# Two message-passing layers on one core: a new opening, wider one-hots, longer rings and VectorE operands in PSUM

## The chip, the cores and the metric

The kernel runs on one core of one Trainium2 chip. The metric is the device time of one execution in microseconds (us), from the start of the program to its end. Of the kernel before, three timed runs and one profiled execution are at hand.

## The reference, cut to what matters

The graph has 12500 nodes of 128 features and 412500 edges, sorted by target. Two layers run one after the other:

```python
deg = maximum(segment_sum(ones, dst), 1.0); d = deg ** -0.5
h = maximum(layernorm(x), 0.0)
msg = where(edge_type == 0, h[src] @ W_data.T + b_data, h[src] @ W_control.T + b_control)
x = x + relu(segment_sum(msg, dst) + h @ W_self.T + b_self)
h = maximum(layernorm(x), 0.0)
g = tanh((h @ gate_w[:D])[dst] + (h @ gate_w[D:])[src] + gate_b)
yn = tanh(edge_weight * yes_weight + (1 - edge_weight) * no_weight)
x = x + segment_sum(h[src] * ((g + yn) * 0.5 * d[dst] * d[src])[:, None], dst)
```

## The kernel before, in words

**Opening.** The nodes are 98 blocks of 128, in 14 chunks of 7 blocks (`CB`). SyncE (SP) loads the chunks of x, and between them the targets (after chunk 2) and the sources (after chunk 3) of the edges, and later their types. For each chunk VectorE takes mean and variance (`stats`), turns them into a scale and a shift (`scales`, L1195, whose L1199 reads two small SBUF tensors), ScalarE applies them (`normal`), TensorE transposes the chunk (`turn`), ScalarE takes the positive part into `HTB`, TensorE multiplies by the self weights (`strip(2)`, L878) and by the two message weights (`strip(4, 256)`, L883), ScalarE puts the self term into the accumulator `ACC` (L664), and VectorE adds the biases into the message rows `YB` (`rows`, L1187, behind `stats` by four chunks). SP stores a chunk of rows to the table `t0` in HBM, and behind each the self terms to `ini`. `YB` has two buffers, so the rows of chunk c wait until those of chunk c - 2 have landed. GpSimd meanwhile computes the indices of the edges (L534 to L562), then waits for the last rows of `t0` and begins to gather.

**Gathers.** An edge tile is 128 edges. Of the 3224 tiles the last 2112 or so are gathered one by one: one indirect DMA issued by GpSimd (L570) brings 128 rows of the table to a ring `G` of 5 slots of 8 tiles. Each layer has 251 items of 8 tiles in a main loop (2008 gathers) and 13 more items (`sections`, 104 gathers) behind it. Before item s GpSimd waits until TensorE has used item s - 5.

**Cells.** The other 1112 tiles are served in another way, in 18 groups of 98 cells (`NG`, `NB`). A cell is a block of 128 source nodes against a window of 256 targets. SP loads the table's rows two cells at a time into a ring (`TC`, `TC1`, 4 places, `RT`) and a row of codes (`RB0`, `RB1`). VectorE compares the codes with the partition number (`pair_hots`, L1290, two operations of 256 columns for two cells; `pair_hots1`, L1747, one of them) and TensorE gathers with that one-hot (`gather`, `gather1`). ScalarE brings the result to SBUF. VectorE makes the one-hot of the targets (`cell_hots`, L1300; `target_hots1`, L1768, two cells in one operation), and TensorE adds the cell into a group's sum (`apply`, `apply1`; in layer 2 in two banks of PSUM in turn), which VectorE adds to `ACC` (L1283, L1787). In layer 2 VectorE also picks for each cell the target's score (`target_score`, L1760: the targets' one-hot times a piece of `ACC`, with an accumulated sum). The constant 0 to 255 that these compare with is `IO16`, int16 in SBUF.

**Items.** For each gathered item VectorE makes a one-hot of 8 x 32 columns (`item_hot`, L1251; `hot1`, L1688, two buffers). In layer 1 it adds the four tiles of a quad for the counts in two steps (L1258, L1260); the `sections` do this by one reduction (L1550). In layer 2 it multiplies the one-hot by scores (L1699), reduces (L1706), adds the source's score (L1715, which waits for the gather), and after ScalarE's tanh weights the one-hot (L1725, L1729). TensorE multiplies, and VectorE adds 32 columns at a time to `ACC` (L1274, L1741).

The order of an engine's work is written out by hand: for each item s, a loop over i mixes the cells `CELL[s]` to `CELL[s+1]` (7 an item) with the item's own steps. Between the layers and at the end the sums are transposed and stored.

Of the kernel before, what the change touches and what calls it, by code (L numbers as in the profile page):

```python
# [5 lines left out]
N = 12500  # L6
D = 128
# [17 lines left out]
NC = NB // CB  # L25

# [26 lines left out]
RT = 4  # L53
# [4 lines left out]
KD1, KX1, KW1 = 6, 6, 8  # L58
# [38 lines left out]
def gnn_program(nc, x, src, dst, d0, g0, typ, ew, w2, ws, bb, bs, gwr, gs, gb, yw, nw, out):  # L97
# [17 lines left out]
    with ctx:  # L115
# [27 lines left out]
        OHT = sb("OHT", [128, TG // QT, 2, W], bf16)  # L143
# [36 lines left out]
        EE = sb("EE", [128, 2, TG])  # L180
        PS = ctx.enter_context(nc.psum_tensor("PS", [128, 8, 512], fp32))
# [4 lines left out]
        def strip(bank, w=128):  # L186
# [24 lines left out]
        HTE += 64 * HB * RT  # L211
        MVF = MV[:, :, :].rearrange("p b a -> p (b a)")
# [8 lines left out]
        OT0 = [a.bitcast(bf16).rearrange("p (a w) -> p a w", a=2)  # L221
               for a in (W2[:, :], OHF[:, 1792:2048], YN[:, HTE:HTE + 256])]
        CD0 = CDST[:, 0:KD * DW // 2].bitcast(bf16).rearrange("p (a w) -> p a w", a=KD)
        OHU = [a[:, 0:2 * NB].bitcast(bf16) for a in (BB, MVF)]
        HTE += 256
# [8 lines left out]
              for a in (HTB[:, :, :, :].rearrange("p a c d -> p (a c d)"), OWF) for n in range(2)]  # L234
# [43 lines left out]
        c_t, c_o = sems("c_t", "c_o")  # L278
# [37 lines left out]

        def passes0(eng):
# [19 lines left out]
        def units(slot, ring=RT):  # L337

            return -(-(NH - slot) // ring)

        def parts_in(c):

            return 16 * units(c % RT) + 32 * (c // RT + 1)

        def pairs_in(c):

            return 16 * units(c % RT) + 32 * (-(-(NG * NH - c % RT) // RT) + c // RT + 1)
# [20 lines left out]
        def _(eng):  # L368
# [3 lines left out]
            for c in range(NC):  # L372
# [6 lines left out]
                if c == 2:  # L379
                    load(STI, dst, s_dst)  # L380
                if c == 3:
                    load(IDX[:, :], src, s_src)
            for c in range(NC):
                if c == 4:
# [3 lines left out]
                eng.wait_ge(a_ye, c + 1)  # L388
# [1494 lines left out]
```

## Time and profile before

| what | value |
|---|---|
| median of 3 runs | 5841.05 us (5840.38 to 5857.13) |
| the profiled execution | 5829.9 us, its span 5828.1 us |
| opening, to the first gather | 0 to 124.4 us |
| layer 1, main loop of gathers | 124.4 to about 2701 us |
| its sections | to about 2853 us |
| between the layers | to about 2963 us |
| layer 2, main loop of gathers | 2963 to about 5628 us |
| its sections, and the end | to 5828 us |
| busy in layer 1 (2576.6 us) | PE 2055.5, DVE 1984.9, ACT 1570.2, POOL 1964.9 us |
| busy in layer 2 (2665.1 us) | PE 1929.8, DVE 2089.7, ACT 1312.9, POOL 2052.2 us |

Busy time of POOL is the time of its instructions; the time between two DMA issues of POOL is written "issue". A stretch's busy time says how full an engine is, not whether the end waits for it. That is read from the waits and from the chain of work that ended last.

### The profile page before, as it was taken

Reading aid. Unit: us, or ns where it says so; the run is one execution under the profiler, and the core shown is the slowest. Engines: PE = TensorE matmul, PEld = TensorE weight load, DVE = VectorE, ACT = ScalarE, POOL = GpSimd, SP = SyncE. Lnnn points to the kernel's source line nnn. Section 1 sums busy time; section 2 is a strip of 40 time slices with the busy share of each in tenths; the row PEclk is TensorE's granted clock in tenths of the full one; section 3 lists DMA queues with packets and bytes.
Section 4 is the critical chain, followed back from the end, with each engine's and each line's share of the span. In section 5 each row is a group of like instructions: output and inputs, shape, how many; then the busy total and the mean of one; then the engine's idle time right before and its main releaser. Section 6 shows DMA issues by size and latency. Waiting matters only on the chain.

```text
span 5828.1 us, 119944 instructions
## 1 busy us (share of the span) xinstructions
PE 4286.3 (74%) x29542; PEld 3197.4 (55%) x29542; DVE 4365.5 (75%) x16525; ACT 3038.4 (52%) x10494; POOL 4307.3 (74%) x4285
## 2 busy tenths in 40 slices
PE   6588888888888888875577777777777777777754
PEld 5355666655565555553455555555555555555543
DVE  7887777878787777755467777777777777777863
ACT  5666666666666666643254544544445444444530
POOL 5777777777777777777457777777777777777774
PEclk8599999999999999987688888888888888888875
DMA  7777777777777777776355455555555455455544
GB/s 239 245 217 223 222 224 223 225 221 223 225 225 224 223 223 222 220 224 203 102 134 121 118 118 119 121 119 120 119 119 121 119 119 119 118 120 118 120 97 116
DMA packets 764988, 979.91 MB, mean 168 GB/s; under 512 B 135667, under 2 KB 567063, under 8 KB 763799
## 3 DMA queue, kind: packets, MB, share of 16 engines
q1 hardware_dynamic: 620131, 687.26, 40.0%
q0 software_dynamic: 135168, 281.42, 19.7%
q8 instruction: 259, 4.24, 0.3%
q10 hardware_dynamic: 9012, 3.56, 0.2%
q14 instruction: 418, 3.42, 0.2%
HBM read 911.05 MB, written 60.67 MB: 167 GB/s over the span
## 4 chain that ended last, share of the span: by engine, by line
POOL 72%; issue 23%; PE 2%; DVE 2%; DMA 1%; SPq 1%; ACTq 0%; DVEq 0%; POOLq 0%; ACT 0%
POOL G L570 72%; SPq L311 1%; PE PS L883 0%; DMA OWF<-in_x 0%; DMA out<-OWF 0%; DVE ST L1172 0%; DVE OHF L1183 0%; DVE G L1639 0%; PE PS L891 0%; DMA G<-t,IDXB 0%; PE PS L1054 0%; PE PS L1057 0%; DVE OWF L1191 0%; DVE OWF L1832 0%; PE PS L1081 0%
## 5 line engine op out<-in xcount | busy, mean ns | idle before, releaser
L570 POOL DMA_INDIRECT G<-t,IDX x4016 | 4019.1, 1001 | 1274.3 <-issue 1223.0
L1081 PE MATMUL PS<-CDST,HTB 128*128 128x256 f32 x2352 | 868.3, 455 | 447.7 <-DVE CDST L1768 419.9
L705 ACT ACTIVATE OHF<-PS 128x384 bf16<-128x384 f32 x1764 | 864.6, 490 | 515.7 <-PE PS L927 488.0
L939 PE MATMUL PS<-CDST,OHF 128*128 128x256 bf16 x5292 | 901.0, 281 | 35.0 <-DVE ACC L1283 35.0
L797 ACT ACTIVATE ST<-PS,MV 128x1 f32<-128x1 f32 x1764 | 457.5, 259 | 720.2 <-issue 327.6
L1072 PE MATMUL PS<-HTB,OWF 128*128 128x129 f32 x3528 | 815.1, 317 | 9.7 <-DVE OWF L1747 9.7
L1072 PEld LDWEIGHTS PS<-HTB,OWF 128*128 128x128 f32 x3528 | 720.5, 218 | 166.8 <-issue 75.9
L1081 PEld LDWEIGHTS PS<-CDST,HTB 128*128 128x128 f32 x2352 | 408.0, 217 | 556.0 <-ACT HTB L816 510.4
L939 PEld LDWEIGHTS PS<-CDST,OHF 128*128 128x128 bf16 x5292 | 532.6, 101 | 315.8 <-issue 68.7
L1081 PE MATMUL PS<-OHF,OWF 128*128 128x256 f32 x1176 | 438.6, 459 | 246.5 <-DVE OHF L1768 230.2
L1300 DVE TENSOR_SCALAR CDST<-IO,BASE 128x256 bf16<-128x256 int16 x1764 | 510.8, 305 | 5.0 <-PE PS L939 4.1
L808 ACT ACTIVATE ST<-ST,BASE 128x1 f32<-128x1 f32 x1764 | 501.1, 284 | 3.0
L958 PE MATMUL PS<-PAY,OWF 128*128 128x196 f32 x1484 | 408.8, 362 | 55.3 <-DVE OWF L1352 47.5
L1760 DVE SCALAR_TENSOR_TENSOR W<-IO,BASE,ACC 128x256 f32<-128x256 int16 x882 | 423.4, 480 | 9.8 <-ACT ST L797 2.9
L816 ACT ACTIVATE HTB<-PS,ST 128x128 f32<-128x128 f32 x1176 | 419.2, 356 | 0.1
L1760 DVE SCALAR_TENSOR_TENSOR BB<-IO,BASE,ACC 128x256 f32<-128x256 int16 x882 | 417.8, 474 | 0.6
L1715 DVE TENSOR_TENSOR SS<-DD,G 128x8 f32<-128x8 f32 x251 | 43.7, 174 | 483.1 <-issue 475.7
L1768 DVE TENSOR_TENSOR CDST<-IO,BASE 128x512 f32<-128x512 int16 x588 | 403.3, 686 | 0.0
L900 PE MATMUL PS<-G,OHF 128*32 128x128 f32 x4016 | 183.5, 305 | 283.0 <-DMA G<-t,IDX 262.8
L1747 DVE TENSOR_SCALAR OWF<-OHF,PCODE 128x256 f32<-128x256 int16 x882 | 347.1, 394 | 36.6 <-DMA HTB<-t 28.8
L1081 PEld LDWEIGHTS PS<-OHF,OWF 128*128 128x128 f32 x1176 | 207.1, 220 | 299.5 <-ACT OWF L816 275.5
L712 ACT ACTIVATE YN<-PS 128x128 f32<-128x128 f32 x251 | 69.7, 278 | 457.8 <-PE PS L906 390.3
(240 smaller groups left out, 8316.9 us busy)
## 6 DMA issues: line engine op xcount, KB each, us to landing
HTB<-t0s SPq DMA_DIRECT2D x442, 384.0 KB
OWF<-t0s SPq DMA_DIRECT2D x440, 384.0 KB
HTB<-t SPq DMA_DIRECT2D x882, 132.0 KB
G<-t,IDX POOLq DMA_INDIRECT x4016
YN<-rows SPq DMA_DIRECT2D x882, 64.0 KB
OHF<-rows SPq DMA_DIRECT2D x882, 64.0 KB
t0s<-HTB SPq DMA_DIRECT2D x25, 384.0 KB
t0s<-OWF SPq DMA_DIRECT2D x24, 384.0 KB
```

Of the source, the lines that this page charges most:

```text
L570: eng.indirect_dma_start(out=G[:, k:k + width], out_offset=None, in_=table, in_offset=bass.IndirectOffsetOnAxis(ap=at, axis=0)).then_inc(s ...
L705: eng.activation(X0[:, k % KX, :, :].rearrange("p n w -> p (n w)"), PS[:, cell_bank(k), 0:384], ACT.Identity).then_inc(q_ev, 1)
L797: eng.activation(TH1[:, k % KW1:k % KW1 + 1], cell_slot(k)[:, D:D + 1], ACT.Tanh, bias=PDE[:, g % 2, b:b + 1]).then_inc(d_th, 1)
L808: eng.activation(WV1[:, n:n + 1], TH1[:, n:n + 1], ACT.Identity, bias=TABS[:, g % 2, PW + b:PW + b + 1]).then_inc(d_w, 1)
L816: eng.activation(X1[k % KX1], cell_slot(k)[:, 0:D], ACT.Identity, scale=WV1[:, n:n + 1]).then_inc(d_ev, 1)
L939: ins = eng.matmul(PS[:, 4, 0:DW], X0[:, k % KX, n, :], CD0[:, k % KD, :], start=b == 0 and n == 0, stop=b == NB - 1 and n == 2)
L958: eng.matmul(PS[:, 7, 0:PW], OHR[t // 2 % KR][:, t % 2, :], PAY[:, t % KP, :], start=j == 0, stop=j == SIZE[g] - 1).then_inc(q_tab, 1)
L1072: eng.matmul(cell_slot(k), OT1[c % RT][:, col:col + 128], TC1[c % RT][:, k % HB, 0:D + 1], start=True, stop=True).then_inc(d_ga, 1)
L1081: eng.matmul(PS[:, 4 + g % 2, 0:DW], X1[k % KX1], CD1[k // 2 % 3][:, k % 2, :], start=b == 0, stop=b == NB - 1).then_inc(d_ap, 1)
L1300: eng.tensor_scalar(CD0[:, k % KD, :], IO16[:, 0:DW], TABS[:, g % 2, NB + b:NB + b + 1], None, ALU.is_equal).then_inc(q_oh, 1)
L1760: eng.scalar_tensor_tensor(JUNK[k % 2], IO16[:, 0:DW], TABS[:, g % 2, NB + b:NB + b + 1], ACC[:, 1, bass.ds(start1[0], DW)], ALU.is_equal, ...
L1768: eng.tensor_tensor(CD1[c % 3], IO16[:, 0:DW].unsqueeze(1).broadcast_to([128, 2, DW]), TABS[:, g % 2, NB + b:NB + b + 2].unsqueeze(2).broa ...
```

## The change

- Opening: chunks are handled in halves of 4 and 3 blocks (`HALF`). The positive part goes to `ACC[:, 0]` (`HT0`) and stays there. The self terms are computed after all messages, from there, with two matmuls of 448 columns a chunk, and stored to `ini` after the last rows of `t0`. `rows` follows `stats` by three chunks, `windows` comes after all rows. The sources are loaded before the targets, the types after chunk 1 of the rows. `scales` copies the means to PSUM (`MP`) and reads them there.
- One-hots of the codes: `quad_hots`, one operation of 512 columns for four cells where there was one of 256 for two, in both layers. In layer 1 the counts come by one `tensor_reduce`.
- Rings: `TC`, `TC1`, `RB0`, `RB1` have 6 places; in layer 2 `CD1` has 5 pairs where it had 3. The space is a new tensor `NX` of 3072 columns; the memory for the descriptors of GpSimd's DMAs goes from its default 16384 to 4096 bytes a partition.
- Layer 2: 0 to 255 stands in PSUM as float32 (`IOP`), and the one-hot of an item too (`OHP`, one buffer, so the next is made after the weighting). The groups' sums use one bank, and VectorE adds them in the cell loop.

```diff
+HALF = ((0, 4), (4, CB))
+RU = 4
+RT = 6
+QC = 4
-KD1, KX1, KW1 = 6, 6, 8
+KD1, KX1, KW1 = 5, 6, 8
+        NX = sb("NX", [128, 3072])
+        HT0 = blocks(ACC[:, 0, 0:NB * 128])
+        MP = PS[:, 2, 0:NB]
+        IOP = PS[:, 5, 0:DW]
+        OHP = PS[:, 5, DW:DW + TG * W].rearrange("p (j w) -> p j w", w=W)
...
             for c in range(NC):
-                if c == 4:
+                if c == 2:
                     eng.wait_ge(s_stg, 1)
                     load(STI, typ, s_typ)
-                eng.wait_ge(a_ye, c + 1)
-                chunk_dma(eng, YB[c % 2], t0, c, False, a_t0[c % 2])
-                if c >= 1:
-                    eng.wait_ge(a_se, c)
-                    eng.dma_start(ini[:, (c - 1) * CB * 128:c * CB * 128],
-                                  ACC[:, 0, (c - 1) * CB * 128:c * CB * 128]).then_inc(s_ini, 16)
+                if c == NC - 2:
+                    eng.wait_ge(s_zr, 1)
+                    eng.dma_start(t0[N:NB * 128, :], ZR[0:NB * 128 - N, :]).then_inc(s_zr, 16)
+                for first, last in HALF:
+                    table_half(c, first, last)
             eng.wait_ge(s_zr, 17)
             for c in (NC - 2, NC - 1):
-                eng.wait_ge(a_t0[c % 2], landed(c, 2))
+                eng.wait_ge(a_t0[c % 2], stored(c))
+            for c in range(NC):
+                eng.wait_ge(a_se, c + 1)
+                eng.dma_start(ini[:, c * CB * 128:(c + 1) * CB * 128],
+                              ACC[:, 0, c * CB * 128:(c + 1) * CB * 128]).then_inc(s_ini, 16)
...
             turn(0)
+            turn(1)
+            for h in range(2 * NC):
+                messages(h)
+                if h + 2 < 2 * NC:
+                    turn(h + 2)
             for c in range(NC):
...
+                if c >= 2:
+                    eng.wait_ge(a_se, c - 1)
+                for n in range(2):
+                    at = c * CB * 128 + n * CB * 64
+                    ins = eng.matmul(PS[:, c % 2 * 2 + n, 0:CB * 64], WS[:, :], ACC[:, 0, at:at + CB * 64],
+                                     start=True, stop=True)
                 ins.then_inc(a_ms, 1)
...
             def scales(c):
                 cols = slice(c * CB, (c + 1) * CB)
                 eng.wait_ge(a_sq, c + 1)
+                eng.tensor_copy(MP[:, cols].unsqueeze(2), MV[:, cols, 0:1])
                 link(eng.reciprocal(RS[:, cols], SQ[:, cols]))
-                eng.scalar_tensor_tensor(DG[:, cols].unsqueeze(2), MV[:, cols, 0:1], -1.0, RS[:, cols].unsqueeze(2),
+                eng.scalar_tensor_tensor(DG[:, cols], MP[:, cols], -1.0, RS[:, cols],
                                          ALU.mult, ALU.mult).then_inc(a_rs, 1)
...
-                quads = OH[:, b, :, :].rearrange("p (q j) w -> p q j w", j=QT)
-                eng.tensor_tensor(OHT[:, :, :, :], quads[:, :, 0:2, :], quads[:, :, 2:4, :], ALU.add).then_inc(m_oh, 1)
-                eng.wait_ge(m_oh, 2 * n)
-                eng.tensor_tensor(OHS[:, b, :, :], OHT[:, :, 0, :], OHT[:, :, 1, :], ALU.add).then_inc(m_os, 1)
+                eng.wait_ge(m_oh, n)
+                with nc.allow_low_precision(reason="counts of at most four"):
+                    eng.tensor_reduce(OHS[:, b, :, :], OH[:, b, :, :].rearrange("p (q j) w -> p q w j", j=QT),
+                                      mybir.AxisListType.X, ALU.add).then_inc(m_os, 1)
...
+            def quad_hots(u):
+                for c in (2 * u, 2 * u + 1):
+                    eng.wait_ge(q_tc[c % RT], parts_in(c))
+                if u >= 3:
+                    eng.wait_ge(q_ga, QC * (u - 2))
                 for t in range(2):
-                    ins = eng.tensor_scalar(OT0[c % 3][:, t, :], RB0[:, c % RT, :], PCODE[:, t:t + 1], None,
+                    ins = eng.tensor_scalar(OT0[:, u % 3, t, :], RB0Q[:, u % 3, :], PCODE[:, t:t + 1], None,
                                             ALU.is_equal)
...
             def hot1(s):
-                if s >= 2:
-                    eng.wait_ge(e_ow, 2 * (s - 1))
+                if s >= 1:
+                    eng.wait_ge(e_ow, 2 * s)
                 t = DT + s * TG
                 eng.tensor_tensor(
-                    OH[:, s % 2, :, :], LOC[:, t:t + TG].unsqueeze(2).broadcast_to([128, TG, W]),
-                    IOTA[:, 0:W].unsqueeze(1).broadcast_to([128, TG, W]), ALU.is_equal).then_inc(e_dd, 1)
+                    OHP, LOC[:, t:t + TG].unsqueeze(2).broadcast_to([128, TG, W]),
+                    IOP[:, 0:W].unsqueeze(1).broadcast_to([128, TG, W]), ALU.is_equal).then_inc(e_dd, 1)
...
-                eng.scalar_tensor_tensor(JUNK[k % 2], IO16[:, 0:DW], TABS[:, g % 2, NB + b:NB + b + 1],
+                eng.scalar_tensor_tensor(JUNK[k % 2], IOP, TABS[:, g % 2, NB + b:NB + b + 1],
                                          ACC[:, 1, bass.ds(start1[0], DW)], ALU.is_equal, ALU.mult,
                                          accum_out=PDE[:, g % 2, b:b + 1]).then_inc(d_pd, 1)
...
-                eng.tensor_tensor(CD1[c % 3], IO16[:, 0:DW].unsqueeze(1).broadcast_to([128, 2, DW]),
+                eng.tensor_tensor(CD1[c % KD1], IOP.unsqueeze(1).broadcast_to([128, 2, DW]),
                                   TABS[:, g % 2, NB + b:NB + b + 2].unsqueeze(2).broadcast_to([128, 2, DW]),
                                   ALU.is_equal).then_inc(d_oh, 1)
...
                     if i < ncell:
                         cell1(k)
+                        if k == (done + 1) * NB + LATE1:
+                            group_add1(done, s - 1)
+                            done += 1
                     if i == 1:
                         score1(s)
-                    if i == 2 and s + 1 < SM:
-                        hot1(s + 1)
-                    if i == 3 and s + 1 < SM:
-                        targets1(s + 1)
                     if i == 4:
                         weight1(s)
+                        if s + 1 < SM:
+                            hot1(s + 1)
+                    if i == 5 and s + 1 < SM:
+                        targets1(s + 1)
...
-    nc = bacc.Bacc("TRN2", target_bir_lowering=False, num_devices=1)
+    nc = bacc.Bacc("TRN2", target_bir_lowering=False, num_devices=1, dynamic_dma_scratch_size=4096)
```

## Rows read from the trace of the kernel before

**Rows 1.** The page: its span, and the chain that ended last, by engine.

```profile
span 5828.1 us, 119944 instructions
...
POOL 72%; issue 23%; PE 2%; DVE 2%; DMA 1%; SPq 1%; ACTq 0%; DVEq 0%; POOLq 0%; ACT 0%
```

**Rows 2.** GpSimd's groups of instructions: main loop of layer 1, then of layer 2.

```profile
L570 POOL DMA_INDIRECT G<-t,IDX x2008 | 1965.9, 979 | 635.9 <-issue 611.9 <-DMA t<-G 23.9
...
L570 POOL DMA_INDIRECT G<-t,IDX x2008 | 2053.2, 1023 | 638.4 <-issue 611.1 <-DMA t<-G 25.5 <-PE PS L900 1.8
```

**Rows 3.** Timeline (start, us, engine, line): layer 2, gathers and VectorE operations of SBUF.

```profile
3072.71 0.35 DVE L1747 TENSOR_SCALAR OWF<-OHF,PCODE 128x256 f32<-128x256 int16 x1
3072.85 1.02 POOL L570 DMA_INDIRECT G<-t,IDX  x1 [0.30 <-issue]
...
4003.88 0.49 DVE L1760 SCALAR_TENSOR_TENSOR W<-IO,BASE,ACC 128x256 f32<-128x256 int16 x1
4003.99 1.20 POOL L570 DMA_INDIRECT G<-t,IDX  x1 [0.30 <-issue]
...
4006.80 0.94 POOL L570 DMA_INDIRECT G<-t,IDX  x1 [0.30 <-issue]
...
4010.16 0.69 DVE L1768 TENSOR_TENSOR OHF<-IO,BASE 128x512 f32<-128x512 int16 x1
4010.55 1.12 POOL L570 DMA_INDIRECT G<-t,IDX  x1 [0.30 <-issue]
```

**Rows 4.** Timeline of layer 1: gathers beside VectorE operations that read PSUM.

```profile
718.09 0.42 DVE L1283 TENSOR_TENSOR ACC<-ACC,PS 128x256 f32 x1
718.26 0.95 POOL L570 DMA_INDIRECT G<-t,IDX  x1 [0.30 <-issue]
...
1618.85 0.29 DVE L1384 SCALAR_TENSOR_TENSOR JK<-WS,PS 98x128 int16<-98x128 f32 x1
1618.90 0.94 POOL L570 DMA_INDIRECT G<-t,IDX  x1 [0.30 <-issue]
```

**Rows 5.** VectorE's groups in layer 2: count, busy, mean ns, idle before.

```profile
L1760 DVE SCALAR_TENSOR_TENSOR W<-IO,BASE,ACC 128x256 f32<-128x256 int16 x881 | 422.9, 480 | 9.8 <-ACT ST L797 2.9 <-DVE OHF L1688 1.2 <-issue 0.9
...
L1768 DVE TENSOR_TENSOR CDST<-IO,BASE 128x512 f32<-128x512 int16 x586 | 402.0, 686 | 0.0
L1747 DVE TENSOR_SCALAR OWF<-OHF,PCODE 128x256 f32<-128x256 int16 x881 | 346.8, 394 | 36.6 <-DMA HTB<-t 28.8 <-PE PS L1072 1.7 <-issue 1.1
...
L1729 DVE TENSOR_TENSOR OWF<-OHF,EE 128x256 f32<-128x256 f32 x250 | 107.0, 428 | 8.6
...
L1715 DVE TENSOR_TENSOR SS<-DD,G 128x8 f32<-128x8 f32 x250 | 43.6, 174 | 482.0 <-issue 474.6 <-DMA G<-t,IDX 6.8
```

**Rows 6.** VectorE's groups in layer 1, and the sections' reduction.

```profile
L1290 DVE TENSOR_SCALAR OHF<-YN,PCODE 128x256 bf16<-128x256 int16 x588 | 148.5, 308 | 118.4 <-DMA OWF<-t0s 60.2 <-DMA HTB<-t0s 54.9 <-PE PS L927 2.5
...
L1258 DVE TENSOR_TENSOR OHT<-OHF 128x128 bf16<-128x128 f32 x390 | 115.2, 295 | 13.3
...
L1550 DVE TENSOR_REDUCE OHS<-OHF 128x64 bf16<-128x256 f32 x13 | 7.6, 587 | 0.4
```

**Rows 7.** Groups of instructions of the first 126 us: messages, and the shift.

```profile
L883 PE MATMUL PS<-W,HTB 128*128 128x256 f32 x196 | 51.0, 416 | 11.8 <-DVE OHF L1191 8.8 <-DVE OWF L1191 2.8
...
L1199 DVE SCALAR_TENSOR_TENSOR SRD<-MV,SRD 128x7 f32<-128x7 f32 x14 | 19.3, 1380 | 0.5
```

**Rows 8.** Timeline of the opening.

```profile
10.96 23.20 SPq L311 DMA_DIRECT2D ACC<-in_x  x11
...
41.10 2.02 DVE L1191 TENSOR_TENSOR OHF<-PS,BB 128x1792 f32<-128x1792 f32 x1 [1.15 <-DMA t<-OHF]
...
84.56 1.44 DVE L1172 BATCH_NORM_STATS2 ST<-ACC 128x6 f32<-128x128 f32 x7
...
86.73 0.17 DVE L1199 SCALAR_TENSOR_TENSOR SRD<-MV,SRD 128x7 f32<-128x7 f32 x1
...
124.41 1.46 POOL L570 DMA_INDIRECT G<-t,IDX  x1 [23.94 <-DMA t<-G]
```

More of the change, by code:

```diff
@@ L378, in _, with table_half @@
                     eng.wait_ge(s_w, 16 * 9)
-                if c == 2:
-                    load(STI, dst, s_dst)
                 if c == 3:
                     load(IDX[:, :], src, s_src)
+                if c == 4:
+                    load(STI, dst, s_dst)
+            def table_half(c, first, last):
+                eng.wait_ge(o_y, 2 * c + 1 + (first > 0))
+                whole = min(last, NB - 1 - c * CB)
+                at = (c * CB + first) * 128
+                eng.dma_start(t0[at:at + (whole - first) * 128, :].rearrange("(b p) w -> p b w", p=128),
+                              YB[c % 2][:, first:whole, :]).then_inc(a_t0[c % 2], 16)
+                if whole < last:
+                    eng.dma_start(t0[(NB - 1) * 128:N, :], YB[c % 2][0:NL, whole, :]).then_inc(a_t0[c % 2], 16)
@@ L645, in normal, with positive @@
                 ins.then_inc(a_n, 1)
+            def positive(c):
+                for n, (first, last) in enumerate(HALF):
+                    eng.wait_ge(o_t, 2 * c + n + 1)
+                    eng.activation(HT0[:, c * CB + first:c * CB + last, :], strip(0)[:, first:last, :], ACT.Relu)\
+                       .then_inc(o_h, 1)
             eng.wait_ge(s_c, 4)
@@ L650, in _ @@
             normal(0)
-            eng.wait_ge(s_w, 16 * 9)
-            for c in range(NC + 1):
+            root(2, 0)
+            positive(0)
+            normal(1)
+            for c in range(1, NC):
                 if c + 2 < NC:
@@ L1187, in rows @@
             def rows(c):
-                eng.wait_ge(a_m, c + 1)
-                if c >= 2:
-                    eng.wait_ge(a_t0[c % 2], landed(c - 2, 2))
-                eng.tensor_tensor(YB[c % 2], strip(4, 256),
-                                  BB[:, :].unsqueeze(1).broadcast_to([128, CB, 256]), ALU.add)\
-                   .then_inc(a_ye, 1)
+                for n, (first, last) in enumerate(HALF):
+                    eng.wait_ge(o_m, 2 * c + n + 1)
+                    if c >= 2 and n == 0:
+                        eng.wait_ge(a_t0[c % 2], stored(c - 2))
+                    eng.tensor_tensor(YB[c % 2][:, first:last, :], strip(4, 256)[:, first:last, :],
+                                      BB[:, :].unsqueeze(1).broadcast_to([128, last - first, 256]), ALU.add)\
+                       .then_inc(o_y, 1)
             def scales(c):
@@ L1206, in _ @@
                     scales(c - 1)
-                if c == 4:
+                if c == 3:
                     eng.wait_ge(s_w, 16 * 9)
-                if c >= 4:
-                    rows(c - 4)
-                if c == NC + 1:
-                    windows()
+                if c >= 3:
+                    rows(c - 3)
+            windows()
             eng.tensor_tensor(YD[:, :], YW[:, :], NW[:, :], ALU.subtract).then_inc(s_bg, 1)
```

276 lines of the change are left out of this document (130 added, 146 removed).

## The prediction

> **What bounds the kernel now.** First the page's chain [rows 1]: 72% of the span is GpSimd's gather instruction and 23% is "issue", the gap that GpSimd needs between two of them. TensorE and VectorE, far busier than they are critical, hold 4% together. So the question for each stretch is what ends GpSimd's own time. The view of its groups in the two main loops answers it [rows 2]: 2008 gathers each, with nothing before them but issue (612 us / 2008 = 0.305 us) and one wait at the start. GpSimd never waits for a ring slot. A layer costs 2008 times the sum of gap and gather, and the gather is 0.979 us in layer 1 and 1.023 in layer 2.
>
> Why are these two not equal? The timeline shows it [rows 3]. An undisturbed gather takes 0.94 us (0.944 is the commonest value). The one at 4003.99 takes 1.20: an L1760 of VectorE that began just before has 0.38 us to go. The one at 4010.55 takes 1.12, with 0.30 us of an L1768 left. Both are longer by what was left less 0.12 us. L1760 and L1768 read two tensors from SBUF. L1747 reads one, yet the gather that it runs into (3072.85, 0.21 left) takes 1.02. Against that [rows 4]: L1283 adds PSUM to SBUF, 0.25 us are left of it, and the gather takes 0.95; L1384, a scalar_tensor_tensor of one SBUF and one PSUM tensor, has 0.24 us left, and the gather takes 0.94. These are the forms that the change gives to L1768 and L1760. Above the floor lie 2008 x 0.035 = 70 us in layer 1 and 2008 x 0.079 = 159 us in layer 2.
>
> A price for one VectorE operation follows. With start times spread evenly over a period P (1.28 or 1.33 us), an operation of length d costs (d - a)^2 / 2P on average. The rows give a = 0.12; an operation must also have begun before the gather asks. I fit a on layer 2: 1761 L1760 of 0.477, 879 L1768 of 0.686, 881 L1747 (0.35 undisturbed), 500 L1729 and L1688 of 0.42 to 0.43 [rows 3, 5] give over 200 us with a = 0.12 and 163 with a = 0.18. The trace has 159, so a = 0.18.
>
> By the Trainium skill (SBUF — State Buffer, "Who interferes with whom"), VectorE operations with two SBUF inputs, and tensor_scalar in its two-port mode, exclude GpSimd from a shared port, while a reduction and operations with one SBUF input outside that mode do not. The trace agrees; the rule also says that the four-cell operations, still tensor_scalar, keep colliding.
>
> **Layer 2.** L1760, L1768, L1688, L1699 and L1729 each lose one SBUF input and fall to nothing. What is left is the four-cell one-hot: 441 of 512 columns instead of 882 of 256. No row has one. Its length lies between 0.35 us (more columns free) and 0.61 (0.26 more, the difference of L1768 and L1729 for 256 columns). I take 0.49: L1290 and L1747 have the same columns and differ by 0.07, so a tensor_scalar's time is not columns at L1768's rate. Price 0.31^2 / 2.5 = 0.038 us, times 441 = 17 us (bounds 5 and 33). With 2 for small things 19 us stay of 159: **-140 us** (-120 to -152).
>
> Does anything else become late? VectorE in layer 2 waits 482 us at L1715 for gathered data, 1.92 us an item of 10.6 [rows 5]. An item becomes 10.05, so 1.4 us of slack stay. Four-cell one-hots take off 882 x 0.39 - 441 x 0.49 = 130 us. PSUM operands I cost at nothing: L1283's 256 columns with PSUM take 0.42 us, as L1729's from SBUF [rows 4, 5]. A table of the Trainium skill (VectorE: DVE Perf Modes, "The TRN2 errata — SBUF-src ops pay a fixed extra latency per instruction") has a fixed 120 cycles instead of 58 for a PSUM source, which would be 0.065 us for each of about 15 operations an item, 1 us: still inside that slack, and no row here shows it. The one buffer for the one-hot adds a wait of VectorE for its own weighting, about 0.1 us. The single bank makes TensorE wait at 17 group ends for VectorE's add (L1283's twin, 0.42 us, and waits): 1 to 2 us each, behind which GpSimd still has four slots, 40 us. Longer rings take at most the 29 us of waits for `HTB` off VectorE, which hides them.
>
> **Layer 1.** Only two things change. L1258 and L1260 (two SBUF inputs) go: 390 x 0.115^2 / 2.56 = -2 us; the reduction that replaces them is longer (0.587 [rows 6]) but has one input. The code one-hots (L1290, three groups of 588; 0.28 us undisturbed, 0.308 mean) become 882 of 512 columns, 0.35 us by the same slope: 882 x 0.011 - 1764 x 0.004 = +3 us (bounds -4 and +38, the latter with 0.54 us). VectorE is relieved by about 200 us in all. The large colliders, L1300, L1321, L1352 and L1251, stay. **+1 us**.
>
> **Opening.** The first gather at 124.41 had waited 23.94 us for the last pieces of `t0` [rows 8]. Ahead of these runs VectorE. SP issues no store before 10.96 + 23.20 = 34.2 us, because eleven loads of x are ahead in its queue; therefore the rows of chunk 2 start at 41.10, waiting for a landing. The change keeps this: same bytes, same queue. After it a chunk takes VectorE 2.34 us from the statistics to the shift (84.56 to 86.90), 2.17 for rows in halves (2.02 plus a second start), 0.25 for copy and waits: 4.75 us. L1199, with a mean of 1.38 us where an undisturbed one takes 0.17 [rows 7, 8], stood for 17 us behind GpSimd's index arithmetic; its PSUM input frees it. From 43.2: eight chunks with statistics (38 us), then three at TensorE's pace (messages 51.0 / 14 = 3.6 us and transposes, 4.3 in all, 13 us), then half a chunk's landing (a whole one took up to 6.9 us, from 34.2 to 41.10, so 3.5): the first gather at **97 us, -27 us**. GpSimd's index arithmetic doesn't come into this: it was done 23.94 us before the first gather, its last step waits for TensorE's last transpose, which moves forward with the rest, and the types are loaded two chunks sooner. Bounds: -40 if the rows never wait, -15 if each chunk keeps 1 us of other waits.
>
> Moved behind it: 28 matmuls, 14 activations, 14 stores of self terms, and on SP behind them the first loads of layer 1's weights and tables. So layer 1's cells start some 20 us after the gathers. VectorE's `windows` (7 us) moves behind the rows too, and its first add waits for the stores. The cover is the five slots of `G`: 40 gathers x 1.25 = 50 us, 40 of them beyond the item in hand. If that cover were gone, the 20 us would come back in full.
>
> **The sum**, against the profiled execution: 5829.9 - 27 + 1 - 140 = 5664. The median of the runs is 11 us above that execution, so the prediction is 5841 - 166 = **5675 us**. About 0.3% (17 us) is what a measurement of this kernel can tell from no change.
>
> **Rivals.**
> - *The early start is given back.* GpSimd begins early but then waits in the fifth item for TensorE, whose cells start late, or the opening is held by something I counted as covered. For it: 20 us of late work, and layer 1's VectorE at 77%. Against: 40 us of slots. 5841 - 139 = 5702 us. Chance 10%.
> - *Layer 2's other engines become the bound.* One one-hot buffer, one bank and VectorE's waits cost over 1.4 us an item, and gathers wait for slots. Half the gain lost: 5841 - 27 - 69 = 5745. Against: the 482 us. It would show as GpSimd waiting for L900. Chance 8%.
> - *PSUM does not help or the code is not what collides.* Only the opening stays: 5814 us. Rows 4 speak against. Chance 3%.
> - *The descriptor memory, a quarter of the former, makes each gather dearer: slower than before.* Place: GpSimd's instruction, 4224 times. GpSimd would have to win space back four times as often. Price: nothing at the low end, one further issue gap of 0.30 us for each gather at the high end. If every fourth gather pays it, 4224 / 4 x 0.30 = 317 us: 5992 us. It decides from 166 / 4224 = 0.039 us a gather. Against: gathers of 0.94 us show no periodic extra now. For: no row shows the small memory. By the Trainium skill (DMA: Bandwidth & Descriptors, "SWDGE vs HWDGE vs iDMA") these descriptors stand in a ring in SBUF that GpSimd writes; what a smaller ring costs it does not say. Chance 5%.
> - My forecast: 74%.
>
> **Range.** 5640 to 5720: layer 2 from -152 to -120, opening from -40 to -15, layer 1 up to +38 at its worst, not all at once, and 8 us of spread between runs. It holds the forecast and the first rival. Faster by over 0.3%: 0.94 (forecast, the first three rivals, less 0.01 for a ring price near the point); within 0.3%: that 0.01; slower: 0.05.
>
> **What would show it.** Gathers of layer 2 at 0.95 us mean (0.944 plus 0.009), those of layer 1 still at 0.98, gaps at 0.305. L1760's and L1768's successors with unchanged durations, and gathers that start beside them at 0.94. The four-cell one-hots near 0.49 and 0.35 us, the small STT of `scales` at 0.17, the first gather near 97 us and no wait for L900 after it. It is wrong if the gather beside a PSUM operand is still lengthened, if the floor of 0.94 or 0.305 moves (the memory), or if GpSimd waits for slots.

## The result and the profile after

The changed kernel takes 5660.19 us (median of 4 runs, 5658.14 to 5662.46) against 5842.56 us of the kernel before in the same comparison (5840.38 to 5857.13): ratio 0.9685, 95% interval 0.9670 to 0.9699, or 182 us. The forecast was 5675 us.

The page of the changed kernel, its span and the chain that ended last [rows 1]:

```profile
span 5660.6 us, 116822 instructions
...
POOL 68%; issue 22%; DVE 3%; PE 3%; DMA 2%; SPq 1%; ACT 1%; DVEq 0%; ACTq 0%; POOLq 0%
```

The spans of the two profiled executions differ by 167.4 us. Cut at the starts of GpSimd's gathers, each main loop from its first gather to its last (us, from the traces):

| stretch | before | after | difference | predicted |
|---|---|---|---|---|
| start to first gather | 124.41 | 106.06 | -18.4 | -27 |
| layer 1's main loop | 2576.8 | 2577.6 | +0.7 | +1 |
| to layer 2's first gather | 261.7 | 262.6 | +0.9 | 0 |
| layer 2's main loop | 2665.1 | 2518.4 | -146.7 | -140 |
| from the last of them to the end | 200.0 | 196.1 | -3.9 | not costed |

GpSimd's groups in the two main loops [rows 2]: count, busy us, mean ns, idle before and what ended it.

```profile
L591 POOL DMA_INDIRECT G<-t,IDX x2008 | 1966.6, 979 | 619.1 <-issue 611.6 <-DMA t<-OWF 7.1 <-PE PS L940 0.3
...
L591 POOL DMA_INDIRECT G<-t,IDX x2008 | 1907.6, 950 | 634.8 <-issue 610.8 <-DMA t<-G 23.1 <-PE PS L934 0.9
```

These lines show three things. The gap is unchanged (612 us / 2008 = 0.305). Layer 1's gather still takes 0.979 us on average. Layer 2's fell from 1.023 to 0.950, and waits for slots stay near nothing (0.3 and 0.9 us). Above the floor of 0.944 lie 71 us in layer 1 (70 before) and 12 us in layer 2 (158 before).

The timeline of layer 2 shows the floor beside the operations that lengthened gathers before [rows 3]:

```profile
3501.33 0.69 DVE L1803 TENSOR_TENSOR CDST<-PS,BASE 128x512 f32<-128x512 f32 x1
3501.40 0.94 POOL L591 DMA_INDIRECT G<-t,IDX  x1 [0.30 <-issue]
...
3506.26 0.47 DVE L1795 SCALAR_TENSOR_TENSOR W<-PS,BASE,ACC 128x256 f32<-128x256 f32 x1
3506.39 0.94 POOL L591 DMA_INDIRECT G<-t,IDX  x1 [0.30 <-issue]
```

The gather at 3501.40 starts with 0.62 us of L1803 left and takes 0.94. VectorE's groups in layer 2 [rows 5] say that these operations did not get shorter; only their place beside GpSimd changed:

```profile
L1795 DVE SCALAR_TENSOR_TENSOR W<-PS,BASE,ACC 128x256 f32<-128x256 f32 x881 | 423.0, 480 | 8.8 <-issue 1.4 <-ACT ST L823 1.3 <-DVE PS L1721 1.2
...
L1803 DVE TENSOR_TENSOR CDST<-PS,BASE 128x512 f32<-128x512 f32 x352 | 241.4, 686 | 0.0
L1781 DVE TENSOR_SCALAR NX<-NX,PCODE 128x512 f32<-128x512 int16 x441 | 223.4, 507 | 7.5 <-DMA HTB<-t 4.4 <-issue 0.6 <-PE PS L1108 0.3
...
L1748 DVE TENSOR_TENSOR SS<-DD,G 128x8 f32<-128x8 f32 x250 | 43.9, 176 | 392.5 <-issue 387.6 <-DMA G<-t,IDX 4.5
```

0.480 and 0.686 us are the lengths of before. Before L1748, which waits for the gathered data, VectorE is idle for 392 us instead of 482; the profile names no releaser for most of it, so that this is the wait for gathers is read from the kernel. Layer 1's groups [rows 6]:

```profile
L1323 DVE TENSOR_SCALAR NX<-YN,PCODE 128x512 bf16<-128x512 int16 x882 | 292.5, 373 | 383.5 <-issue 171.0 <-DMA OWF<-t0s 77.5 <-DMA HTB<-t0s 73.9
L1289 DVE TENSOR_REDUCE OHS<-OHF 128x64 bf16<-128x256 f32 x390 | 232.9, 597 | 13.3
```

The opening's timeline [rows 8], with the one very long gather that follows it; then the shift's small operation [rows 7], and VectorE's waits for messages (L903 after, L883 before: total us, times, longest):

```profile
12.35 22.79 SPq L319 DMA_DIRECT2D ACC<-in_x  x10
...
41.19 2.09 DVE L1227 TENSOR_TENSOR OHF<-PS,BB 128x1024 f32<-128x1024 f32 x2 [11.48 <-DMA t<-OHF]
...
106.06 1.17 POOL L591 DMA_INDIRECT G<-t,IDX  x1 [7.13 <-DMA t<-OWF]
...
112.72 3.52 DVE L1201 TENSOR_TENSOR LOC<-DST,DS 128x3224 int16<-128x3224 int16 x1
113.00 4.05 POOL L591 DMA_INDIRECT G<-t,IDX  x1 [0.30 <-issue]
```

```profile
L1236 DVE SCALAR_TENSOR_TENSOR SRD<-PS,SRD 128x7 f32<-128x7 f32 x14 | 2.3, 166 | 0.5
```

```profile
DVE OWF L1227 <- PE PS L903: 14.8, 11, 3.0
...
DVE OHF L1227 <- PE PS L903: 5.1, 4, 2.1
```

```profile
DVE OWF L1191 <- PE PS L883: 10.5, 4, 4.9
...
DVE OHF L1191 <- PE PS L883: 6.3, 3, 3.1
```

Rows of chunk 2 start at 41.19, as forecast, but the last rows end at 102, 61 us later and not some 53. The shift takes 0.166 us a piece instead of 1.38, as forecast: 17 us less of VectorE's time. How the 18 us divide between this and the other edits of the opening was not tested.

The gather at 113.00 starts with 3.24 us left of L1201, an operation with two SBUF inputs that the change moved behind the start. It takes 4.05 us: 3.24 - 0.12 + 0.94, the relation of the short operations.

### The profile page after: what moved, and what is told of

Read it like the earlier page. It is cut to its first block, busy times and chain, and to the rows that moved or that the text cites. A ratio compares the mean times of both kernels' runs of the same rounds, so it can differ in the third digit from the quotient of the medians.

```text
span 5660.6 us, 116822 instructions
## 1 busy us (share of the span) xinstructions
PE 4293.0 (76%) x29402; PEld 3188.3 (56%) x29402; DVE 4220.0 (75%) x14841; ACT 3040.9 (54%) x10508; POOL 4161.8 (74%) x4285
## 3 DMA queue, kind: packets, MB, share of 16 engines
q14 instruction: 395, 3.24, 0.2%
## 4 chain that ended last, share of the span: by engine, by line
POOL 68%; issue 22%; DVE 3%; PE 3%; DMA 2%; SPq 1%; ACT 1%; DVEq 0%; ACTq 0%; POOLq 0%
POOL G L591 68%; SPq L319 1%; PE PS L903 0%; DMA HTB<-ini 0%; PE PS L925 0%; PE PS L917 0%; DMA OWF<-in_x 0%; DMA out<-OWF 0%; DVE ST L1207 0%; PE PS L1117 0%; DMA G<-t,IDXB 0%; DVE CDST L1447 0%; DMA G<-t,IDX 0%; ACT ACC L664 0%; DVE OHF L1447 0%
## 5 line engine op out<-in xcount | busy, mean ns | idle before, releaser
L731 ACT ACTIVATE OHF<-PS 128x384 bf16<-128x384 f32 x1764 | 864.6, 490 | 414.2 <-PE PS L962 385.8
L1108 PE MATMUL PS<-HTB,NX 128*128 128x129 f32 x3528 | 806.0, 314 | 10.8 <-DVE NX L1781 10.8
L1108 PEld LDWEIGHTS PS<-HTB,NX 128*128 128x128 f32 x3528 | 710.5, 215 | 166.7 <-issue 81.8
L1117 PE MATMUL PS<-CDST,OWF 128*128 128x256 f32 x1416 | 528.8, 459 | 177.0 <-ACT OWF L842 144.3
L842 ACT ACTIVATE OWF<-PS,ST 128x128 f32<-128x128 f32 x1764 | 629.9, 357 | 0.2
L1323 DVE TENSOR_SCALAR NX<-YN,PCODE 128x512 bf16<-128x512 int16 x882 | 292.5, 373 | 383.5 <-issue 171.0
L1333 DVE TENSOR_SCALAR CDST<-IO,BASE 128x256 bf16<-128x256 int16 x1764 | 495.7, 305 | 39.1 <-PE PS L974 38.4
L934 PE MATMUL PS<-G,OHF 128*32 128x128 f32 x4016 | 176.3, 296 | 341.7 <-DMA G<-t,IDX 326.1
L1795 DVE SCALAR_TENSOR_TENSOR W<-PS,BASE,ACC 128x256 f32<-128x256 f32 x882 | 423.5, 480 | 8.8 <-issue 1.4
L1795 DVE SCALAR_TENSOR_TENSOR BB<-PS,BASE,ACC 128x256 f32<-128x256 f32 x882 | 420.7, 477 | 3.1 <-issue 0.5
L1117 PEld LDWEIGHTS PS<-CDST,OWF 128*128 128x128 f32 x1416 | 244.8, 216 | 249.0 <-ACT OWF L842 199.9
L1117 PE MATMUL PS<-NX,OWF 128*128 128x256 f32 x704 | 262.1, 458 | 102.4 <-ACT OWF L842 82.5
L1748 DVE TENSOR_TENSOR SS<-DD,G 128x8 f32<-128x8 f32 x251 | 44.1, 176 | 393.0 <-issue 388.2
L934 PEld LDWEIGHTS PS<-G,OHF 128*32 128x32 f32 x4016 | 106.3, 115 | 406.3 <-issue 363.6
L1117 PE MATMUL PS<-OWF 128*128 128x256 f32 x704 | 262.6, 458 | 89.5 <-ACT OWF L842 71.2
```

What stands on the lines that cost most here:

```text
L731: eng.activation(X0[:, k % KX, :, :].rearrange("p n w -> p (n w)"), PS[:, cell_bank(k), 0:384], ACT.Identity).then_inc(q_ev, 1)
L842: eng.activation(X1[k % KX1], cell_slot(k)[:, 0:D], ACT.Identity, scale=WV1[:, n:n + 1]).then_inc(d_ev, 1)
L1108: eng.matmul(cell_slot(k), OT1[:, k // QC % 3, col:col + 128], TC1[c % RT][:, k % HB, 0:D + 1], start=True, stop=True).then_inc(d_ga, 1)
L1117: eng.matmul(PS[:, 4, 0:DW], X1[k % KX1], CD1[k // 2 % KD1][:, k % 2, :], start=b == 0, stop=b == NB - 1).then_inc(d_ap, 1)
L1323: ins = eng.tensor_scalar(OT0[:, u % 3, t, :], RB0Q[:, u % 3, :], PCODE[:, t:t + 1], None, ALU.is_equal)
L1333: eng.tensor_scalar(CD0[:, k % KD, :], IO16[:, 0:DW], TABS[:, g % 2, NB + b:NB + b + 1], None, ALU.is_equal).then_inc(q_oh, 1)
```

## Experiments

Times are medians; ratios are to the kernel before on the same chip. "Excess" is a main loop's sum of gather times above 0.944 us, put down to the VectorE operation that is running when the gather starts. The edits are cut to what matters.

### One operand back in SBUF, and rings of four: a chip with another bound

```diff
-JUNK[k % 2], IOP, TABS[...]                     # L1795, score_sbuf
+JUNK[k % 2], IO16[:, 0:DW], TABS[...]
-CD1[c % KD1], IOP.unsqueeze(1)...               # L1803, targets_sbuf
+CD1[c % KD1], IO16[:, 0:DW].unsqueeze(1)...
```

`all_sbuf` has both, and the items' one-hot (with its constant) in SBUF (`OHF`) instead of `PS`. `rings_of_four` has RT = 4, rings of four tables (and `u % 2` for the quads' slots; a quad is four cells).

> The changed kernel, with the constant 0..255 of target_score (L1795) read from SBUF as int16 again, all else as changed. Theory (an operation with two SBUF tensor inputs holds up the gather that starts beside it; price (d - 0.18)^2 / 2P a piece): 1764 x (0.478 - 0.18)^2 / 2.55 = 61 us, so +50 to +65 us, mean gather of layer 2 0.950 -> 0.978, all the new excess beside L1795, its own length unchanged at 0.48. Rival (the gain of layer 2 came from the longer rings, the four-cell one-hots or the descriptor memory, and the place of the operands is worth little): 0 to +10 us.

> The changed kernel, with the constant of target_hots1 (L1803) read from SBUF again, all else as changed. Theory: 882 x (0.686 - 0.18)^2 / 2.55 = 89 us, so +75 to +92 us, mean gather of layer 2 0.950 -> 0.990. Rival (a price in proportion to busy time: 603 us of L1803 here against 845 of L1795, so less than the score's): under +45 us. Rival (place worth little): 0 to +10 us.

> The changed kernel, with every operand of layer 2's VectorE work in SBUF again (the constants of L1795 and L1803, and the targets' one-hot, still one buffer). Theory: the two prices above add up, and the one-hot, its products and its weighting add some 13: +140 to +163 us, layer 2's gathers at 1.02 us mean. That is the whole of layer 2's gain. Rival (rings and four-cell one-hots carry a part): under +120 us. Rival (not additive, since a gather that is late already hides the next operation): under +130 us.

> The changed kernel with RT = 4: rings of four tables and code rows in both layers, four-cell one-hots kept. Theory (no engine but GpSimd is on the path): 0 us, within 8, though VectorE's waits for landed tables at L1323 and L1781 grow by an order of magnitude, since a quad's second table can start to load only when the quad before it is gathered; no wait of GpSimd for slots. Rival (the longer rings are what lets the others keep up): +20 us or more, with GpSimd waiting for L934 and L940.

Measured: 7553.8, 7545.7, 7435.9 and 7800.0 us, while the kernel before took 7620.2 (ratios 0.991, 0.990, 0.976 and 1.024). On this chip GpSimd is not the bound. TensorE's granted clock is 0.78: the upper of its two levels in 55% of the time of `score_sbuf`, against 74% in the changed kernel's first trace (0.87). And TensorE's results come late. Timeline of `score_sbuf` in layer 1:

```profile
1496.84 0.49 PE L962 MATMUL PS<-NX 128*128 128x384 bf16 x2
...
1500.16 0.48 PE L962 MATMUL PS<-NX 128*128 128x384 bf16 x2 [2.17 <-issue]
...
1503.81 0.49 ACT L731 ACTIVATE OHF<-PS 128x384 bf16<-128x384 f32 x1 [3.27 <-remote]
...
1504.35 0.82 PE L962 MATMUL PS<-NX 128*128 128x384 bf16 x2 [3.38 <-ACT OHF L731]
```

Counted through the layer, the L731 at 1503.81 fetches the result of the L962 at 1496.84, whose modelled end is 1497.32: it starts 6.5 us later. The L962 at 1500.16 is the next cell's. Of the L731 between 1000 and 2000 us that start after a wait of over 0.3 us, a quarter start over 4.9 us behind their matmul's modelled end. In the changed kernel's first trace all of these start 0.04 us behind it. GpSimd's group in layer 1 there:

```profile
L591 POOL DMA_INDIRECT G<-t,IDX x2008 | 1939.0, 966 | 1801.3 <-PE PS L940 1208.4 <-issue 537.7 <-remote 48.0
```

1208 us of waits for TensorE: the times of these four say nothing for or against the theory. The gathers do: layer 2's excess is 45 us with L1795's constant in SBUF, 54 with L1803's, 151 with everything, and 11 with everything in PSUM (`rings_of_four`). The single prices, 37 us beside L1795 and 50 beside L1803 where 61 and 89 were forecast, are low because fewer gathers start beside these operations: 371 and 267, against 492 and 428 in `all_sbuf_again` below, at the same 0.10 and 0.19 us each. Why `all_sbuf` was the fastest of these four was not settled. The changed kernel itself wasn't measured on this chip.

### The whole of layer 2 back in SBUF, and layer 1 into PSUM

`as_changed` is the changed kernel; `all_sbuf_again` is as above. `layer1_psum`:

```diff
+IOQ = PS[:, 6, 0:128]          # 0..127, copied from IO16 before windows()
+OWQ = PS[:, 6, 128:256]        # 16384..16511, likewise
-IOTA[:, 0:W] (L1284); IO16[:, 0:NB] (L1354); IO16[:, DW:DW + 128] (L1385)
+IOQ[:, 0:W];          IOQ[:, 0:NB];          OWQ
-to = PS[:, 5 + q % 2, 0:n * NB]; eng.wait_ge(q_rk, q - 1)
+to = PS[:, 5, 0:n * NB];         eng.wait_ge(q_rk, q)
-RANKLAG = 5; KR = 3
+RANKLAG = 3; KR = 4            # fourth buffer: W2
```

> The changed kernel itself, once more, as the measure for the kernels beside it, since the first four experiments ran on a chip on which every kernel took about 7500 us and GpSimd waited for TensorE. Where TensorE keeps up (kernel before near 5840 us): 5660 us, ratio 0.9685. On a chip where TensorE is what GpSimd waits for: theory (what the change takes off GpSimd then no longer sets the time) a ratio between 0.97 and 1.00, with the mean gather of layer 2 still at 0.950 us; rival (the longer rings are worth most where the waits are) below 0.97.

> Every operand of layer 2's VectorE work in SBUF again, as in all_sbuf. Where GpSimd is the bound: theory +140 to +163 us over the changed kernel, layer 2's gathers at 1.02 us mean; rival (rings and four-cell one-hots carry a part) under +120 us.

> The changed kernel with layer 1's constants in PSUM too: 0..127 and 16384..16511 as fp32 in bank 6, read by L1284, L1354 and L1385 in place of SBUF constants; the ranks then have bank 5 alone, are read two tiles sooner, and have four buffers of one-hots behind them. Theory (two SBUF inputs are what lengthens a gather): in the changed kernel 19 us of layer 1's excess lie beside L1354, 19 beside L1385 and 8 beside L1284; they go, and 25 us of excess stay (the one-hots of L1323 and L1333, the opening's L1201): 71 -> 25 us, mean gather 0.979 -> 0.957, -46 us where GpSimd is the bound. Rival (the price in layer 1 belongs to the DMA load, 220 GB/s against 126 in layer 2, not to the operands): 0 to -10 us. Rival (one bank for the ranks makes TensorE wait for VectorE's reduction at each of 290 units): gathers cheaper, but waits of GpSimd for L940 take it back, 0 us or slower.

| | time (us) | ratio, 95% | excess layer 1 | excess layer 2 |
|---|---|---|---|---|
| `as_changed` | 5657.9 | 0.9690 (0.9668 to 0.9713) | 63 | 14 |
| `all_sbuf_again` | 5804.3 | 0.9940 (0.9922 to 0.9959) | 78 | 165 |
| `layer1_psum` | 5611.4 | 0.9612 (0.9589 to 0.9635) | 24 | 12 |

GpSimd's group and VectorE's in layer 2 of `all_sbuf_again`:

```profile
L591 POOL DMA_INDIRECT G<-t,IDX x2008 | 2060.8, 1026 | 640.0 <-issue 611.4 <-DMA t<-G 28.0 <-PE PS L934 0.6
```

```profile
L1803 DVE TENSOR_TENSOR CDST<-IO,BASE 128x512 f32<-128x512 int16 x352 | 242.1, 688 | 0.0
```

The same operation takes 0.688 us from SBUF and 0.686 from PSUM; layer 2's gathers cost 152 us more. The time rises by 146.4 us: all of layer 2's gain is the operands' place. By operation the excess is 81 us beside L1803, 49 beside L1795, 8 beside L1721, 7 beside L1732 and 3 beside L1762 (15 stay beside L1781). The price rule said 89 and 61 for the first two, and up to 163 in all: it overrates them by 8 and 12 us.

Layer 1 of `layer1_psum`, GpSimd's group and a stretch of its timeline:

```profile
L593 POOL DMA_INDIRECT G<-t,IDX x2008 | 1919.1, 956 | 619.0 <-issue 611.6 <-DMA t<-OWF 7.1 <-PE PS L942 0.3
```

```profile
1004.89 0.57 DVE L1359 TENSOR_TENSOR YN<-PS,YN 128x392 bf16<-128x392 f32 x1 [0.72 <-ACT PAY L717]
1005.16 0.94 POOL L593 DMA_INDIRECT G<-t,IDX  x1 [0.30 <-issue]
...
1018.85 0.42 DVE L1390 TENSOR_TENSOR W<-PS,BASE 128x256 f32<-128x256 f32 x1
1018.96 0.94 POOL L593 DMA_INDIRECT G<-t,IDX  x1 [0.30 <-issue]
```

Both gathers start with 0.3 us of the operation left and take 0.94. The time falls by 46.5 us where -46 was expected, and 24 us of excess stay where 25 were. That the fall is met so closely is in part luck: it was worked out from the 71 us of the first trace, while `as_changed` beside it has 63, so only 40 of the 49 us between the two profiled executions lie in layer 1's gathers; 4 lie between the layers and 5 elsewhere, unexplained. The theory carries to a layer whose DMA traffic is almost twice as high (223 GB/s against 126), and the single bank for ranks costs GpSimd nothing (0.3 us of waits for L942). The rivals of both experiments fall.

### The opening

`store_among_loads`; `rows_one_later` has this and the second edit; `best` has both and `layer1_psum`.

```diff
+if c == 9:  table_half(0, *HALF[0]); table_half(0, *HALF[1])   # in SP's loop of x loads
+if c == 11: table_half(1, *HALF[0]); table_half(1, *HALF[1])
-for c in range(NC + 3): ... if c >= 3: rows(c - 3)             # VectorE
+for c in range(NC + 4): ... if c >= 4: rows(c - 4)
```

> The changed kernel with the first two chunks' stores of t0 issued by SP between its loads of x (behind those of chunks 9 and 11) instead of behind all fourteen. Theory (the 11.5 us that VectorE waits at the rows of chunk 2 are SP's queue, and everything behind them moves up): rows of chunk 2 at 30 us instead of 41, first gather at 91 to 94 us instead of 102 to 106, -9 to -12 us in all. Rival (the opening is paced by what the DMA engines carry, 220 to 250 GB/s, so the wait only moves to later chunks): first gather within 3 us of the changed kernel's. Rival (the held back loads of x come late): VectorE waits at its statistics, slower.

> The same, and VectorE shifts and copies the rows of a chunk one chunk later (four behind its statistics instead of three). Theory (a chunk takes 5.8 us and not the 4.75 of VectorE's own work because VectorE waits for messages that TensorE could only start when ScalarE had normalized the next chunk: 20 us of waits for L903): these waits fall under 5 us, the pace to 4.8 to 5.0 us a chunk, first gather 7 to 10 us before that of the run beside it. Rival (the ring ScalarE - TensorE - ScalarE itself needs 5.8 us a chunk): same first gather, the wait moves to L1210 or L1207.

> Both edits of the opening and layer 1's constants in PSUM. Theory (separate stretches of GpSimd's queue, so the gains add): 5658 - 46 - 11 - 8 = 5593 us, ratio 0.957. Rival (an earlier start is given back in layer 1, whose cells start after the self terms): GpSimd waits for L936 or L942 in the first 20 items, 5611 us.

| | first gather (us) | time (us) | ratio, 95% | excess layer 1 |
|---|---|---|---|---|
| `as_changed` | 102.2 | 5657.9 | 0.9690 (0.9668 to 0.9713) | 63 |
| `store_among_loads` | 99.0 | 5660.9 | 0.9688 (0.9670 to 0.9706) | 79 |
| `rows_one_later` | 95.2 | 5658.2 | 0.9679 (0.9659 to 0.9700) | 79 |
| `best` | 94.2 | 5605.2 | 0.9592 (0.9575 to 0.9610) | 29 |

Timeline of `store_among_loads`:

```profile
27.11 2.77 SPq L388 DMA_DIRECT2D t<-OHF  x2
...
34.56 2.09 DVE L1233 TENSOR_TENSOR OHF<-PS,BB 128x1024 f32<-128x1024 f32 x2 [5.61 <-DMA t<-OHF]
...
48.94 2.09 DVE L1233 TENSOR_TENSOR OHF<-PS,BB 128x1024 f32<-128x1024 f32 x2 [4.32 <-DMA t<-OHF]
```

The wait at chunk 2 is halved, and 4.3 us of it come back at chunk 4: its rows wait until those of chunk 2 have landed, whose store stands behind the last loads. Moving stores within a queue that is full of loads until 39 us moves the wait: the rows of chunk 2 start at 34.6 us where 30 was expected, and 3 of the expected 9 to 12 us are gained at the first gather. In `rows_one_later` the waits of VectorE in the first 102 us are:

```profile
DVE ST L1213 <- DMA ACC<-in_x: 8.9, 4, 3.8
DVE OHF L1233 <- DMA t<-OHF: 6.9, 2, 5.7
DVE OWF L1233 <- PE PS L909: 5.5, 6, 1.4
DVE OHF L1233 <- PE PS L909: 3.2, 4, 1.3
```

Waits for messages fall from 15.6 us (11.2 + 4.4 in `as_changed`) over 13.2 (`store_among_loads`) to 8.7; the later rows alone take off 4.5. Under 5 us in all were expected. Between 60.97 and 73.95 us rows follow each other every 4.33 us, where the same chunks take 5.3 in `store_among_loads`. Over chunks 4 to 9 the pace is 4.8 us, and 4.8 to 5.0 were expected. So these waits set the pace there. The first gather comes 3.8 us earlier than in the run beside it, where 7 to 10 were expected: the waits for landed stores (L1233 <- DMA t) still take 6.9 us.

Neither moves the time by an amount that can be measured: 5661 and 5658 against 5658 us. `best` was expected at 5593 us and took 5605, 6 us under `layer1_psum`, and the intervals overlap. GpSimd's waits for slots in its layer 1 are 0.3 us, so the rival, an early start that is given back in such waits, fails too, though its 5611 us is the nearer number. The start's 3 and 7 us are smaller than the spread of layer 1's excess, which is 63, 71, 78, 79 and 79 us in five executions that have the same layer 1. The spread would come from where VectorE's operations fall beside the gathers, since nothing else differs in the layer; whether an earlier start pushes it up can't be said from these runs.

### Rings of four again, and pairs with rings of four

`rings_of_four_again` is RT = 4 alone. `pairs_and_rings_of_four` also has QC = 2, with one chunk of two cells per one-hot (L1323 and L1781 on 256 columns).

> The changed kernel with rings of four tables, where GpSimd is the bound (the first run of it fell on the chip of 7500 us and had no measure beside it). Theory: 0 us, within 8; VectorE's waits before L1323 and L1781 grow several times over, GpSimd's gathers stay at 0.98 and 0.950 us and don't wait for L934 or L940. Rival: slower by 20 us or more, with such waits.

> The changed kernel with both the four-cell one-hots and the longer rings undone (two cells per operation, QC = 2, and rings of four tables), PSUM operands, opening and counts as changed. Rings of four with four-cell one-hots cost 600 us, all of it in layer 1, so the two edits belong together; what are they worth as a pair? Theory (VectorE, relieved of some 340 us, is on no path; the collisions of 1764 + 882 short operations cost what those of 882 + 441 long ones do): within 10 us of 5660, layer 2's excess 12 us again, layer 1's 63 to 79, the range of the same code in the runs so far. Rival (layer 1's first items or layer 2's shorter item need VectorE's relief): +20 us or more, with waits of GpSimd for L934 or L940. Rival (short operations collide less, as the prediction had it): 8 to 15 us faster.

6261.4 us (ratio 1.0726, 1.0701 to 1.0752) and 5672.9 us (0.9690, 0.9674 to 0.9706). Layer 1 of the first, GpSimd's group, and the waits of the same stretch (total, times, longest):

```profile
L591 POOL DMA_INDIRECT G<-t,IDX x2008 | 1962.0, 977 | 1162.3 <-PE PS L940 605.7 <-issue 549.5 <-DMA t<-OWF 7.1
```

```profile
ACT OHF L731 <- PE PS L962: 1079.1, 1093, 7.6
POOL G L591 <- PE PS L940: 605.7, 205, 9.4
...
DVE NX L1323 <- issue: 388.7, 147, 7.6
DVE NX L1323 <- DMA OWF<-t0s: 326.4, 105, 10.2
DVE NX L1323 <- DMA HTB<-t0s: 307.9, 116, 7.3
```

My expectation was wrong by 600 us. Of the 581 us between this profiled execution and that of `as_changed`, 546 are layer 1's main loop and 34 lie between the layers. The expectation's first half is right: VectorE's waits at L1323 rise from 384 to 1043 us. But VectorE works in order, and the one-hots of layer 1's items and cells stand behind the waiting operation. In the changed kernel a quad lasts 2577.6 / 441 = 5.84 us, of which VectorE works 75%, 4.4 us, and a table takes some 5.1 us from SP's issue to its landing. With four slots a quad's second table is issued only when the quad two before has been gathered. 3116 / 441 = 7.07 us a quad is what was measured; it was not worked out from these terms. In layer 2 the landing takes 3.4 us, and its main loop stays at 2524 us.

With pairs the ring of four suffices: the waits at L1323 are 369 us,

```profile
L1323 DVE TENSOR_SCALAR NX<-YN,PCODE 128x256 bf16<-128x256 int16 x1764 | 447.7, 310 | 368.6 <-DMA HTB<-t0s 183.3 <-DMA OWF<-t0s 173.9 <-PE PS L962 8.6
```

and GpSimd doesn't wait. So the longer rings are what the four-cell one-hots need, and the two together are worth 0 to 15 us: the ratios are equal (0.9690 both), the medians, on two chips, 15 us apart. Of the 16 us between the profiled execution and that of `as_changed` 15 are layer 1's excess, 78 us against 63, within the spread above. That excess does shift, with 16 us beside L1333 instead of 4.

## Why the prediction held, and where it did not

- **The bound and the floor.** Right. Gap and floor are unchanged, so a change in a layer's time is a change in its excess. The rival on the descriptor memory falls: its rule decides from 0.039 us a gather, and 0.944 and 0.305 us did not move.
- **Layer 2.** Right: -147 for -140. The four-cell term was a little too high: beside L1781 lie 10 to 16 us where I had 17. Beside L1803, L1795 and the rest lie 2 where I kept 2. The operations that I had fall to nothing did, which the reverse experiment confirms with 146 us.
- **Lengths.** 0.507 and 0.373 us for the four-cell one-hots against 0.49 and 0.35; the reduction 0.597 against 0.587. PSUM operands cost nothing in length: 0.480 and 0.686 us unchanged, with int16 in SBUF replaced by float32 in PSUM. A table of the Trainium skill (VectorE: DVE Perf Modes, "The TRN2 errata — SBUF-src ops pay a fixed extra latency per instruction") has 120 fixed cycles for a PSUM source against 58, 0.065 us more by my estimate from it; the traces don't show it.
- **Layer 1.** Right, +0.7 for +1, in part by luck: five executions of the same layer 1 spread over 16 us. L1201 added 3.1 us that I had not listed, though my text moves `windows` behind the rows.
- **Opening.** Mis-sized, -18 for -27. The step that failed is VectorE's 4.75 us a chunk, with 0.25 us for the copy and all waits. The first trace has 5.7 us from chunk 2 to chunk 10: VectorE waits 19.9 us in all for messages, since TensorE can start those of a chunk only when ScalarE has taken its positive part, and ScalarE does that behind the normalization of the next chunk. The kernel before had 16.8 us of these waits already; a pace read from one chunk without them left them out. With the rows one chunk later the pace reaches 4.33 us for three chunks, which supports this cause. My bound of -15 ("if each chunk keeps 1 us of other waits") was the better description. The first trace is also a late one: in nine others with this opening the first gather comes at 101.4 to 103.3 us (102.2 in `as_changed`, with 15.6 us of such waits), 5 us behind the forecast and not 9.
- **Given back.** The rival did not happen: TensorE's work on the gathered rows (L934) ends up to 21 us behind the last gather of its item in the first fourteen items (10 before), under the 40 us of slots, and GpSimd waits 0.3 us in the whole main loop. The lag is 5.5 us by item 40.
- **Layer 2's other engines.** Did not become the bound: 0.9 us of waits for L934.
- **The rings.** Predicted harmless, with at most 29 us off VectorE. As a pair with the four-cell one-hots they are worth 0 to 15 us; that the latter can't stand without them I did not see.
- **The sum.** Against the profiled execution I had 5664 us; the profiled execution after took 5662.5. That this is met within 1.5 us is luck in part: the opening fell short by 9 us, layer 2 gave 7 more and the end, which I had not costed, 4. The 11 us between the profiled execution and the median of before, which I added, don't exist after: its four runs lie within 4.3 us. They are most of the 15 us by which the forecast missed.

Parted by stage, the 182 us are 147 in layer 2 (the operands' place), 18 of opening, 4 of the end, 0 of rings, one-hots and counts, and 15 the different distance of the profiled execution from its median (12.7 us before, -2.3 after), against 1.6 us lost in layer 1 and between the layers. Layer 2's share was tested by undoing its cause, and the rings with the one-hots by undoing both; the opening's was not.

`layer1_psum` (5611 us) and `best` (5605 us) beat both kernels. What stays of layer 1's excess in `layer1_psum` is 24 us, 9.5 beside the one-hots of L1323 and L1333 and 9 beside the 98 subtractions that split the table (49 each at L1444 and L1447 of the changed kernel).

## What to carry to other kernels

Where GpSimd's gathers set the pace, price VectorE's operations by what they do to a gather that starts beside them: an operation with two tensor inputs in SBUF held the gather up until it ended, one with an input in PSUM did not, and both were equally long. The ring that feeds an engine which works in order has to be counted in batches of what one of its operations waits for, not in tiles. A gain in the opening of a few us can't be seen when the main loop's collisions spread by 16.

## What was not expected of the hardware

- The same kernel before had medians of 5837, 5844 and 5854 us on three chips and 7620 us on a fourth. There TensorE's granted clock was 0.78, and ScalarE fetched results up to 7 us after their modelled ends. What holds them is open.
- A gather that starts beside a 3.52 us operation of VectorE with two SBUF inputs took 4.05 us: up to this length the runs show no limit of the hold.
- Identical code in layer 1 had 63 to 79 us of excess, so what the collisions cost is not a constant of the code.
